# Cross-attention layer: keys and queries of a head in every fourth partition, filled by 7 transfers over 128 partitions

## The chip, the cores and the metric

The kernel runs on 1 core of one Trainium2 chip. The metric is the device time of one execution in microseconds (us), as the median of several runs. Engines: TensorE (PE, its weight loads PEld), VectorE (DVE), ScalarE (ACT), GpSimd (POOL) and SyncE (SP). SP and ScalarE each issue DMA transfers on a queue of their own; the 16 DMA engines serve both.

## The reference

One layer of cross-attention with an MLP: 8 batches of 256 queries and 1601 keys, width 256, 16 heads of width 16, all in f32.

```
x = layer_norm(hidden, ln1_w, ln1_b)
q = heads(x @ q_w + q_b); k = heads(ctx @ k_w + k_b); v = heads(ctx @ v_w + v_b)
attn = softmax(where(mask, q k^T / sqrt(16), -max))
hidden = merge(attn v) @ cproj_w + cproj_b + hidden
out = hidden + gelu(layer_norm(hidden, ln2_w, ln2_b) @ fc_w + fc_b) @ proj_w + proj_b
```

## The kernel before, in words

*Split products.* Keys and queries are held as a high part that TensorE's short format (fp32r) represents exactly and a low rest. A score is q_hi k_hi + q_hi k_lo + q_lo k_hi, which one product makes if the three terms are stacked along the contraction: 3 x 16 rows. Two rows come on top: row 48 (MASKROW) adds the mask (ones among the queries, the mask's large negative number among the keys), row 49 (MAXROW) subtracts a bound of the row's maximum (ones among the keys, minus the sampled maximum among the queries).

*Slots.* A batch has 4 slots (SLOTS) of 4 heads. `kst` [128, 4 slots, 2, 1664] and `qst` [128, 4 slots, 2, 256] hold them: heads j = 0, 1 of a slot in partitions 0 to 49, heads j + 2 in partitions 64 to 113 (HALF = 64), so that the products of two heads use the two halves of TensorE's array. Both are SBUF tensors; the other partitions are not used.

*The way of the keys.* k_unit multiplies a chunk of the context (4 chunks of 384, 384, 384 and 449 keys) by the key weights into a PSUM bank, for two groups of 8 heads (mt = 0, 1). k_evac on VectorE (lines 725 and 728) makes the high and low part in kpart. store_k on SP (line 386) writes them to k_scr in HBM: 4 stores per group of heads, 384 or 449 KB each. q_evac and store_q (line 392) do the same for the queries. `fill` then reads a slot from k_scr and q_scr into kst and qst: in each half, 32 partitions of keys (hi and lo, line 348), 16 partitions of keys (hi again, line 349), 1 partition of mask (line 351), 32 partitions of queries (hi twice, by a broadcast of 2 copies) and 16 of queries (lo, both line 355): 10 transfers in all (FILLS). The order of heads and widths in k_scr is set on the host by `by_width`, which reorders the columns of the weights.

*The maxima.* max_unit (line 1106) multiplies a sample of queries with a sample of keys of a slot, 49 rows deep; it waits for the slot's fill (slot_in). VectorE reduces it (lines 771, 774), turns it to rows (line 785), and SP sends the rows to MAXROW of qst (send_rows, line 398, 4 transfers). Only then may the scores of this slot begin.

*The stream.* For each batch 52 steps (STEPS = 4 slots x 13 tiles of 128 keys), in 26 pairs: scores (line 1119, 4 products per step, 50 rows deep, into S), ScalarE's exponential (line 583, 128 x 1024 into pr), values (line 1126). Between them, at pairs given in tables (K_AT, V_AT, MAX_AT, Q_AT and others), TensorE makes the next batch's keys, values and queries (line 1056, 1093) and the maxima. Slots 2 and 3 of batch 0 have their sampled products at pairs 3, 5, 9 and 11 of batch 0 itself; slot 0 and 1 ahead of the stream.

*Order in the head.* Each engine runs a list written by hand. SP: loads, the mask, six transfers of constant rows (constant_rows, lines 407 to 411: mask rows beyond key 1601, ones of MAXROW in kst, ones of MASKROW in qst), store_k(0, 0, 0 to 3), store_q(0), half 0 of slot 0's fill, store_k(0, 1, 0 to 3), rows of slots 0 and 1, slot 3's fill, then per batch. ScalarE: copies of the context to its high part (line 571), the loads of batch 1's context (next_ctx, line 340), half 1 of slot 0's fill, slot 1's fill, slot 2's fill, then the exponentials. A fill of batch 0 (first_fill) waits for the stored queries (q_out), for the stored keys of its group (k_landed: the 4 stores of mt = 0 for slots 0 and 1, all 8 for slots 2 and 3), for the mask and the constant rows. GpSimd: small memsets (line 494: the columns of kst beyond key 1601), c_low (line 515), c_high of later batches (line 510).

A second run of the whole computation stands under `failed(...)`, for maxima that proved too low; it isn't entered here.

Of the kernel before, what the change touches and what calls it, by code (L numbers as in the profile page):

```python
# [42 lines left out]
H, HD = 16, 16  # L43
# [17 lines left out]
CHUNK = [c for c in range(CH) for _ in range(NT[c])]  # L61
HALF = P // 2
NJ = HG // 2
MASKROW, MAXROW = 3 * HD, 3 * HD + 1
KROWS = MAXROW + 1
SCALE = 1.0 / float(np.sqrt(HD))
EPS = 1e-5
# [106 lines left out]
def build(nc, x, ctx_t, mask, w_kv, w_qc, fc, pj, cols, rows, ident, out):  # L174
    stack = ExitStack()
    with stack:
# [3 lines left out]
        def sem(name):  # L180
            return stack.enter_context(nc.semaphore(name))
# [95 lines left out]
        ln_steps, ln_root = sem("ln_steps"), sem("ln_root")  # L277
        good_steps, good_ready, flag_done = map(sem, ("good_steps", "good_ready", "flag_done"))
        xn_done, xb_done, xagain_done = map(sem, ("xn_done", "xb_done", "xagain_done"))
        o_zeroed, again_zeroed = sem("o_zeroed"), sem("again_zeroed")  # L280
        mlpw_hi, mlpw_lo = sem("mlpw_hi"), sem("mlpw_lo")

        kb_ready, kb_taken, mb_ready, mb_taken, xb_ready, xb_taken = map(
# [56 lines left out]
            eng.dma_start(cT[:, c, :, 0:NK[c]], ctx_t[b, :, :, T0[c] * P:T0[c] * P + NK[c]].rearrange("k p t -> p k t")  # L340
                          ).then_inc(ctx_in[c], 16)

        def fill(eng, s_, b, s, halves=range(2)):

            rows_of = k_scr[bass.ds(b, 1), s // 2].rearrange("o r (d h) t -> (o r d) h t", h=HM)
            for g_ in halves:
                r0, h0 = g_ * HALF, HG * (s % 2) + NJ * g_
                eng.dma_start(kst_d[r0:r0 + 2 * HD, s, :, 0:LK], rows_of[:, h0:h0 + NJ, 0:LK]).then_inc(s_.slot_in[s], 16)
                eng.dma_start(kst_d[r0 + 2 * HD:r0 + 3 * HD, s, :, 0:LK], rows_of[0:HD, h0:h0 + NJ, 0:LK]
                              ).then_inc(s_.slot_in[s], 16)  # L350
                eng.dma_start(kst_d[r0 + MASKROW:r0 + MASKROW + 1, s, :, 0:LK],
                              mask_scr[bass.ds(b, 1), :].unsqueeze(1).broadcast_to([1, NJ, LK])
                              ).then_inc(s_.slot_in[s], 16)
                for r, copies in ((0, 2), (1, 1)):
                    eng.dma_start(qst_d[r0 + 2 * HD * r:r0 + 2 * HD * r + copies * HD, s, :, :].rearrange("p j q -> p (j q)"),
                                  q_scr[bass.ds(b, 1), s // 2, r].rearrange("o (d h) q -> o d (h q)", h=HM)[
                                      :, :, h0 * LQ:(h0 + NJ) * LQ].broadcast_to([copies, HD, NJ * LQ])
                                  ).then_inc(s_.slot_in[s], 16)

        FILLS = 10  # L360
        ROWS_IN = 16 * HG

        def k_landed(eng, units):
# [3 lines left out]

        UK = 2 * CH

        def first_fill(eng, b, s, halves=range(2)):  # L370

            eng.wait_ge(q_out, 32 * (b + 1))
            k_landed(eng, UK * b + CH * (s // 2 + 1))
            if b == 0:
                eng.wait_ge(mask_out, 16)
                eng.wait_ge(ones_in, 16 * 6)
            else:
                eng.wait_ge(first.scores_done, STEPS * (b - 1) + KT * (s + 1))
            fill(eng, first, b, s, halves)

        @block.sync
        def _(sp):
            def store_k(b, mt, c):
                u, t, n = UK * b + CH * mt + c, T0[c] * P, NK[c]
                sp.wait_ge(kb_taken, k_use(b, mt, c) + 1)
                sp.dma_start(k_scr[b, mt, :, :, t:t + n].rearrange("r p t -> p r t"),
                             kpart[:, u % KBUF, :, 0:n].bitcast(F32)).then_inc(k_out[u % KBUF], 16)

            def store_q(b):
                sp.wait_ge(ql_done, b + 1)  # L390
                for mt in range(2):
                    sp.dma_start(q_scr[b, mt].rearrange("r p q -> p r q"), qpart[:, mt, :, :].bitcast(F32)
                                 ).then_inc(q_out, 16)
# [11 lines left out]
            def constant_rows():  # L405
                for r0 in (0, HALF):
                    sp.dma_start(kst_d[r0 + MASKROW:r0 + MASKROW + 1, :, :, LK:KP].rearrange("p s j t -> p (s j) t"),
                                 ones[0:1, 0:KP - LK].unsqueeze(1).broadcast_to([1, SLOTS * NJ, KP - LK])).then_inc(ones_in, 16)
                    sp.dma_start(kst_d[r0 + MAXROW:r0 + MAXROW + 1, :, :, :].rearrange("p s j (n t) -> p (s j n) t", t=P),
                                 ones[1:2, 0:P].unsqueeze(1).broadcast_to([1, SLOTS * NJ * KT, P])).then_inc(ones_in, 16)  # L410
                    sp.dma_start(qst_d[r0 + MASKROW:r0 + MASKROW + 1, :, :, :].rearrange("p s j t -> p (s j) t"),
                                 ones[1:2, 0:LQ].unsqueeze(1).broadcast_to([1, SLOTS * NJ, LQ])).then_inc(ones_in, 16)
# [13 lines left out]
            sp.wait_ge(some_out, 16)  # L426
            sp.dma_start(some[:], some_scr[0].partition_broadcast(P)).then_inc(some_in, 16)

            sp.wait_ge(pads_set, 3)
            constant_rows()  # L430

            for c in range(CH):
                store_k(0, 0, c)
            store_q(0)
            first_fill(sp, 0, 0, [0])
            for c in range(CH):
                store_k(0, 1, c)
            first_rows(0, 0)
# [31 lines left out]
            with failed(sp):  # L470
                for s in range(SLOTS):
                    sp.sem_inc(whole.mrow_in[s], ONE)
                sp.wait_ge(pads_set, 11)
                constant_rows()
                sp.wait_ge(ones_in, 16 * 12)
                sp.dma_start(hid[:], x.rearrange("n p d -> p n d")).then_inc(xagain_in, 16)
                with sp.Fori(0, B) as b:
                    sp.wait_ge(whole.h_steps, ONE + b)
                    for s in range(SLOTS):
                        fill(sp, whole, b, s)  # L480
                        sp.dma_start(vsl[:, 0, s, :, :].rearrange("p t w -> p (t w)"),
                                     v_scr[bass.ds(b, 1), :, s, :].rearrange("o p w -> (o p) w")).then_inc(whole.slot_in[s], 16)
                    for s in range(SLOTS):
                        sp.wait_ge(max_taken, ONE + USES * (SLOTS * b + s + 1))
                        send_rows(whole, b, s)
                store_out(whole)

        @block.gpsimd
        def _(pool):
# [1 line left out]
            nc.gpsimd.memset(ones[:], 1.0).then_inc(pads_set, 1)  # L491
            pool.wait_ge(pads_set, 1)
            nc.gpsimd.memset(ones[0:1, :], -MASKED).then_inc(pads_set, 1)
            nc.gpsimd.memset(kst_d[:, :, :, LK:KP], 0.0).then_inc(pads_set, 1)
            nc.gpsimd.memset(cT[:, CH - 1, :, NK[-1]:NKM], 0.0).then_inc(pads_set, 1)

            def v_pads(par, before):
# [55 lines left out]
            y_low(first)  # L553
            with failed(pool):
                pool.wait_ge(first.pj_ready, TOK)
                nc.gpsimd.memset(kst_d[:, :, :, LK:KP], 0.0).then_inc(pads_set, 1)
                pool.wait_ge(xagain_in, 16)
                nc.gpsimd.tensor_tensor(hid[:], hid[:], bc_s.unsqueeze(1).broadcast_to([P, TOK, D]), ALU.add
                                        ).then_inc(xagain_done, 1)
                y_low(whole)  # L560

        @block.scalar
        def _(act):
# [5 lines left out]
            def high(c):  # L569
                act.wait_ge(ctx_in[c], 16)  # L570
                nc.scalar.activation(c_hi[:, c, :, 0:NKE[c]], cT[:, c, :, 0:NKE[c]], ACT.Copy).then_inc(hi_done, 1)  # L571
# [59 lines left out]
            x_root(0, 2 * QT, XA_VAR)  # L631
            for c in range(2, CH):
                high(c)
            for c in range(CH):
                next_ctx(1, c)
            first_fill(act, 0, 0, [1])
            first_fill(act, 0, 1)
            first_fill(act, 0, 2)
            for b in range(B):
# [411 lines left out]
        def _(pe):  # L1051
# [45 lines left out]
            def max_unit(b, s, j, kb, mb):  # L1097

                if j == 0:
                    pe.wait_ge(first.slot_in[s], 16 * FILLS * (b + 1))  # L1100
                bank_free(mb_taken, mb)
                bank_free(kb_taken, kb)
                for q in range(QT):
                    for g_, (bank, ready) in enumerate(((MB[:, :], mb_ready), (KB, kb_ready))):
                        rows_ = slice(g_ * HALF, g_ * HALF + MASKROW + 1)
                        last = nc.tensor.matmul(bank[:, q * SAMPLE:(q + 1) * SAMPLE], query_set(rows_, s, j, q),  # L1106
                                                kst[rows_, s, j, q * SAMPLE:(q + 1) * SAMPLE], start=True, stop=True)
                        if q == QT - 1:
                            last.then_inc(ready, 1)
# [173 lines left out]
            def all_maxima(n, b, s):  # L1283
                pe.wait_ge(whole.slot_in[s], 16 * (FILLS + 1) * (b + 1))
                for h in range(HG):
                    g_, j = h // NJ, h % NJ
                    rows_ = slice(g_ * HALF, g_ * HALF + MASKROW + 1)
                    for i, (q, k, w) in enumerate(ALLKEYS):
                        pe.wait_ge(max_taken, ONE + USES * n + h * len(ALLKEYS) + i)
                        nc.tensor.matmul(MB[:, 0:w], query_set(rows_, s, j, q), kst[rows_, s, j, k:k + w],  # L1290
                                         start=True, stop=True).then_inc(max_ready, 1)
# [64 lines left out]
```

## Time and profile before

| | us |
|---|---|
| median of 3 runs | 773.13 |
| lowest and highest | 768.25, 775.28 |
| the profiled execution | 768.76 |
| its span, first to last instruction | 767.0 |
| PE busy in it | 702.5 (92%) |
| PEld busy | 478.5 (62%) |
| ACT busy | 446.1 (58%) |
| DVE busy | 371.3 (48%) |
| POOL busy | 120.9 (16%) |

Queue q1 (SP) moved 80.47 MB in 40700 packets, q10 (ScalarE) 32.17 MB in 10494. How to read it: busy time of PE is modelled, and a share over the whole span is a mean over stretches with different limits. PEclk is the clock granted to TensorE as a share of 2.4 GHz, so 0.50 is 1.2 GHz. The DMA share is the mean over 16 engines. Lines named Lnnn are those of the kernel below; "SPq" and "ACTq" are issues of DMA transfers. "idle before ... <-X" says what ended an engine's idle time.

### The profile page before, as it was taken

How to read it: one execution, taken by the hardware profiler on the slowest of the kernel's cores; microseconds unless marked ns; L12 is line 12 of the kernel's file. 1: busy time of each engine (PE TensorE's matmuls, PEld its weight loads, DVE VectorE, ACT ScalarE, POOL GpSimd, SP SyncE). 2: the span in 40 equal slices, each digit the busy share in tenths (PEclk: the TensorE clock that was granted, in tenths of full speed). 3: DMA queues.
4: the chain of work that ended last, by engine and by line, in shares of the span. 5: the costliest groups of instructions: out<-in, count | busy, mean ns of one | idle time of the engine just before them, and what ended most of it. 6: DMA issues, size and time to landing. Idle time of an engine off the chain costs nothing.

```text
span 767.0 us, 16866 instructions
## 1 busy us (share of the span) xinstructions
PE 702.5 (92%) x7026; PEld 478.5 (62%) x7026; DVE 371.3 (48%) x824; ACT 446.1 (58%) x475; POOL 120.9 (16%) x90
## 2 busy tenths in 40 slices
PE   3657699899999999999999999999998978999997
PEld 3545466566656656666566566656664544597897
DVE  6643355265436534643464446534642331467663
ACT  3004366856676677567756775676566788733321
POOL 5222002200220032003201220131000600110010
PEclk9867799999999999999999999999999989999999
DMA  9787578657874788477938694878475800000000
GB/s 312 216 186 131 186 184 188 179 138 183 189 203 128 174 188 217 143 180 158 235 123 203 148 246 123 192 153 230 132 165 126 253 6 2 1 21 8 29 28 31
DMA packets 51275, 113.78 MB, mean 148 GB/s; under 512 B 7050, under 2 KB 40178, under 8 KB 49914
## 3 DMA queue, kind: packets, MB, share of 16 engines
q1 hardware_dynamic: 40700, 80.47, 44.5%
q10 hardware_dynamic: 10494, 32.17, 13.8%
q8 instruction: 58, 0.95, 0.6%
q14 instruction: 23, 0.19, 0.1%
HBM read 65.30 MB, written 47.06 MB: 146 GB/s over the span
## 4 chain that ended last, share of the span: by engine, by line
PE 76%; ACT 13%; DMA 5%; DVE 3%; issue 2%; ACTq 1%; DVEq 0%
PE O L1126 21%; PE S L1119 16%; ACT pr L583 11%; PE O L1056 10%; PE XB L1056 10%; PE O L1213 6%; PE S L1056 6%; DMA k_scr<-kpart 2%; DMA qst<-q_scr 2%; PE XB L1093 2%; PE XB L1153 2%; PE MB L1106 2%; DVE kpart L725 1%; DVE kpart L728 1%; DMA cols_s<-in_cols 1%
## 5 line engine op out<-in xcount | busy, mean ns | idle before, releaser
L583 ACT ACTIVATE pr<-S 128x1024 f32<-128x1024 f32 x416 | 400.6, 1024 | 188.6 <-PE S L1119 184.4
L1126 PE MATMUL O<-pr,vsl 128*17 128x256 f32 x3328 | 227.4, 388 | 1.3 <-DVE ot L790 1.3
L1119 PEld LDWEIGHTS S<-qst,kst 50*128 50x128 f32 x1664 | 117.1, 188 | 120.4 <-ACT pr L583 81.4
L1119 PE MATMUL S<-qst,kst 50*128 50x256 f32 x1664 | 171.7, 315 | 18.7 <-ACT pr L583 15.0
L1126 PEld LDWEIGHTS O<-pr,vsl 128*17 128x17 f32 x3328 | 75.3, 97 | 79.2 <-issue 17.7
L725 DVE TENSOR_SCALAR kpart<-O,cols_s 128x384 fp32r<-128x384 f32 x64 | 40.6, 635 | 120.7 <-PE O L1056 120.7
L771 DVE TENSOR_REDUCE mx<-MB 128x2 fp32r<-128x512 f32 x64 | 44.1, 690 | 79.0 <-PE MB L1106 79.0
L510 POOL CAST c_hi<-cT 128x768 fp32r<-128x768 f32 (+1 forms) x28 | 23.9, 852 | 348.0 <-DMA cT<-in_ctx_t 235.8
L1056 PE MATMUL XB<-w_hi,c_hi 128*128 128x256 f32 (+1 forms) x208 | 68.3, 328 | 2.1 <-DVE vsl L739 1.3
L739 DVE TENSOR_TENSOR vsl<-XB,rows_s 128x256 f32<-128x256 f32 (+1 forms) x104 | 43.3, 417 | 55.1 <-PE XB L1056 55.1
L1056 PE MATMUL O<-c_hi,w_hi 128*128 128x384 f32 (+1 forms) x128 | 52.6, 411 | 17.7 <-POOL c_lo L515 10.3
L515 POOL TENSOR_TENSOR c_lo<-cT,c_hi 128x768 fp32r<-128x768 f32 (+1 forms) x32 | 60.9, 1904 | 8.9 <-ACT c_hi L571 6.7
L1056 PE MATMUL XB<-w_lo,c_hi 128*128 128x256 f32 (+1 forms) x208 | 60.5, 291 | 0.0
L1056 PE MATMUL XB<-w_hi,c_lo 128*128 128x256 f32 (+1 forms) x208 | 60.1, 289 | 0.0
L601 ACT ACTIVATE g<-S,cols_s 128x512 f32<-128x512 f32 x32 | 22.1, 690 | 57.1 <-PE S L1056 52.8
L790 DVE STREAM_TRANSPOSE ot<-O 128x256 f32<-128x256 f32 x32 | 14.4, 450 | 78.0 <-PE O L1126 77.2
L1056 PEld LDWEIGHTS XB<-w_hi,c_hi 128*128 128x128 f32 (+1 forms) x208 | 40.1, 193 | 17.3 <-issue 9.0
L1056 PE MATMUL O<-c_lo,w_hi 128*128 128x384 f32 (+1 forms) x128 | 45.7, 357 | 0.0
L1056 PE MATMUL O<-c_hi,w_lo 128*128 128x384 f32 (+1 forms) x128 | 45.5, 355 | 0.0
L1106 PE MATMUL MB<-kst,qst 49*128 49x256 f32 x128 | 29.8, 314 | 16.3 <-DMA qst<-q_scr 16.2
L774 DVE TENSOR_REDUCE mx<-O 128x2 fp32r<-128x512 f32 x64 | 43.6, 682 | 0.0
L728 DVE SCALAR_TENSOR_TENSOR kpart<-O,cols_s,kpart 128x384 fp32r<-128x384 f32 x64 | 40.6, 635 | 2.3
(100 smaller groups left out, 825.6 us busy)
## 6 DMA issues: line engine op xcount, KB each, us to landing
kst<-k_scr SPq DMA_DIRECT2D x59, 400.2 KB
k_scr<-kpart SPq DMA_DIRECT2D x48, 384.0 KB, 8.0
v_scr<-vsl ACTq DMA_DIRECT2D x8, 1768.0 KB, 11.9
kst<-k_scr SPq DMA_DIRECT2D x59, 200.1 KB
cT<-in_ctx_t ACTq DMA_DIRECT2D x21, 384.0 KB, 7.6
k_scr<-kpart SPq DMA_DIRECT2D x16, 449.0 KB, 7.1
q_scr<-qpart SPq DMA_DIRECT2D x16, 256.0 KB, 2.5
qst<-q_scr SPq DMA_DIRECT2D x59, 64.0 KB
```

Of the source, the lines that this page charges most:

```text
L515: nc.gpsimd.tensor_tensor(c_lo[:, c, :, 0:n], cT[:, c, :, 0:n], c_hi[:, c, :, 0:n].bitcast(F32), ALU.subtract).then_inc(lo_done, 1)
L583: nc.scalar.activation(pr[:, n % PBUF, :], S[:, 2 * (n % 2):2 * (n % 2) + 2, :] .rearrange("p a n -> p (a n)"), ACT.Exp).then_inc(s_.exp_d ...
L725: nc.vector.tensor_scalar(kpart[:, i, 0, 0:n], KB[:, 0:n], bk_s[:, mt:mt + 1], None, ALU.add).then_inc(kh_done, 1)
L728: nc.vector.scalar_tensor_tensor(out=kpart[:, i, 1, 0:n], in0=KB[:, 0:n], scalar=bk_s[:, mt:mt + 1], in1=kpart[:, i, 0, 0:n].bitcast(F32), ...
L739: nc.vector.tensor_tensor(vsl[0:m, b % 2, :, kt, :].rearrange("p s (h w) -> p s h w", w=VW)[:, :, :, 0:HD], XB[0:m, 0:D].rearrange("p (s h ...
L771: nc.vector.tensor_reduce(mx[:, s % 2, :, j], MB[:, :].rearrange("p (q k) -> p q k", q=QT), AX.X, ALU.max, negate=True).then_inc(mb_taken, 1)
L774: nc.vector.tensor_reduce(mx[:, s % 2, :, NJ + j], KB.rearrange("p (q k) -> p q k", q=QT), AX.X, ALU.max, negate=True).then_inc(kb_taken, 1)
L1056: last = nc.tensor.matmul(dst, a, c, start=i == 0, stop=i == len(terms) - 1)
L1106: last = nc.tensor.matmul(bank[:, q * SAMPLE:(q + 1) * SAMPLE], query_set(rows_, s, j, q), kst[rows_, s, j, q * SAMPLE:(q + 1) * SAMPLE], ...
L1119: last = nc.tensor.matmul(S[:, 2 * (n % 2) + g_, j * LQ:(j + 1) * LQ], kst[rows_, s, j, kt * P:(kt + 1) * P], qst[rows_, s, j, :], start=T ...
L1126: last = nc.tensor.matmul(O[32 * h:32 * h + VW, 0, 0:LQ], vsl[:, par, s, kt, h * VW:(h + 1) * VW], pr[:, n % PBUF, h * LQ:(h + 1) * LQ], s ...
L1213: last = nc.tensor.matmul(O[:, n % 2, 0:D], w[:, i, cut], v[:, i, :], start=i == 0 and m == 0, stop=i == NI - 1 and m == 2)
```

## The change

The three parts of keys and queries no longer stand one behind the other. A half array's partition 4 d + part holds dimension d of part 0, 1 or 2 (PARTS = 4), the two halves together every fourth partition of all 128. Part 3's partitions are zero but for two: partition 3 of a half is MASKROW, partition 63 MAXROW. A fill is 3 transfers of 32 partitions for the keys, 3 for the queries and 1 of two partitions for the mask. The products are 64 rows deep (sampled ones 63). For the zeros GpSimd clears all of qst (2048 columns) where it cleared the last columns of kst (504), and ScalarE writes kst by 8 copies of 1664 zeros from qst; SP's constant rows wait for them and go behind store_k(0, 0, 0 to 3). SP issues two of slot 0's transfers and ScalarE the five others, where each issued a half.

```diff
-MASKROW, MAXROW = 3 * HD, 3 * HD + 1
+PARTS = HALF // HD
+MASKROW, MAXROW = PARTS - 1, HALF - 1
 KROWS = MAXROW + 1
...
+        def fill_k(eng, s_, b, s, parts):
+            rows_ = slice(HALF * (s % 2), HALF * (s % 2 + 1))
+            for part in parts:
+                eng.dma_start(kst_d[part::PARTS, s, :, 0:LK],
+                              k_scr[bass.ds(b, 1), s // 2, part % 2, rows_, 0:LK].rearrange("o (p j) t -> (o p) j t", j=NJ)
                               ).then_inc(s_.slot_in[s], 16)
+        def fill_q(eng, s_, b, s):
+            rows_ = slice(HALF * (s % 2), HALF * (s % 2 + 1))
+            for part, r in enumerate((0, 0, 1)):
+                eng.dma_start(qst_d[part::PARTS, s, :, :].rearrange("p j q -> p (j q)"),
+                              q_scr[bass.ds(b, 1), s // 2, r, rows_, :].rearrange("o (p j) q -> (o p) (j q)", j=NJ)
                               ).then_inc(s_.slot_in[s], 16)
+        def fill_mask(eng, s_, b, s):
+            eng.dma_start(kst_d[MASKROW::HALF, s, :, 0:LK],
+                          mask_scr[bass.ds(b, 1), :].unsqueeze(1).broadcast_to([2, NJ, LK])).then_inc(s_.slot_in[s], 16)
+        def fill(eng, s_, b, s):
+            fill_k(eng, s_, b, s, range(PARTS - 1))
+            fill_q(eng, s_, b, s)
+            fill_mask(eng, s_, b, s)
-        FILLS = 10
+        FILLS = 7
...
@@ sync
-            sp.wait_ge(pads_set, 3)
-            constant_rows()
             for c in range(CH):
                 store_k(0, 0, c)
+            sp.wait_ge(pads_set, 3)
+            sp.wait_ge(kst_zeroed, SLOTS * NJ)
+            constant_rows()
             store_q(0)
-            first_fill(sp, 0, 0, [0])
+            fill_ready(sp, 0, 0)
+            fill_k(sp, first, 0, 0, [0, 1])
...
@@ gpsimd
-            nc.gpsimd.memset(kst_d[:, :, :, LK:KP], 0.0).then_inc(pads_set, 1)
+            nc.gpsimd.memset(qst_d, 0.0).then_inc(pads_set, 1)
...
@@ scalar
             for c in range(2, CH):
                 high(c)
+            zeros = qst_d.rearrange("p s j q -> p (s j q)")[:, 0:KP]
+            for s in range(SLOTS):
+                for j in range(NJ):
+                    nc.scalar.activation(kst[:, s, j, :], zeros, ACT.Copy).then_inc(kst_zeroed, 1)
             for c in range(CH):
                 next_ctx(1, c)
-            first_fill(act, 0, 0, [1])
+            fill_ready(act, 0, 0)
+            fill_k(act, first, 0, 0, [2])
+            fill_q(act, first, 0, 0)
+            fill_mask(act, first, 0, 0)
             first_fill(act, 0, 1)
             first_fill(act, 0, 2)
...
@@ tensor, sampled products
-                        rows_ = slice(g_ * HALF, g_ * HALF + MASKROW + 1)
+                        rows_ = slice(g_ * HALF, g_ * HALF + MAXROW)
...
@@ host
     def by_width(a):
-        return a.reshape(*a.shape[:-1], 2, HM, HD).swapaxes(-1, -2).reshape(a.shape)
+        return a.reshape(*a.shape[:-1], H // NJ, NJ, HD).swapaxes(-1, -2).reshape(a.shape)
```

## Rows read from the trace of the kernel before

**Rows 1.** Stretches: length, busy us (PE, PEld, DVE, ACT, POOL), PE clock, DMA share, GB/s
```profile
0.00:83.00 83.00, 43.25 (x244) 35.76 (x244) 39.14 (x78) 16.40 (x17) 24.67 (x28) 0.81 0.82 208
83.00:95.00 12.00, 12.00 (x98) 7.93 (x98) 6.33 (x12) 3.99 (x5) 0.00 (x0) 0.74 0.53 208
95.00:665.00 570.00, 551.64 (x6074) 349.46 (x6073) 262.50 (x605) 396.48 (x413) 89.03 (x59) 0.99 0.65 161
```

**Rows 2.** Sum of waits: total us, times, longest us
```profile
PE MB L1106 <- DMA qst<-q_scr: 16.2, 3, 6.7
```

**Rows 3.** TensorE in order of time, 44 to 84 us: start, us
```profile
49.61 0.58 PE L1106 MATMUL MB<-kst,qst 49*128 49x256 f32 x1 [5.38 <-DMA qst<-q_scr]
...
60.70 0.58 PE L1106 MATMUL MB<-kst,qst 49*128 49x256 f32 x1 [4.16 <-DMA qst<-q_scr]
...
65.24 0.81 PE L1119 MATMUL S<-qst,kst 50*128 50x256 f32 x8
...
75.46 0.74 PE L1119 MATMUL S<-qst,kst 50*128 50x256 f32 x8
82.88 0.58 PE L1106 MATMUL MB<-kst,qst 49*128 49x256 f32 x1 [6.68 <-DMA qst<-q_scr]
```

**Rows 4.** Chain that ended last, 40 to 84 us: start, us, what
```profile
42.84 18.23 DMA k_scr<-kpart
...
61.31 0.32 ACTq L348
...
66.17 16.66 DMA qst<-q_scr
```

**Rows 5.** ScalarE in order of time: start, us
```profile
5.98 1.54 ACT L628 ACTIVATE pr<-pr 8x1601 f32<-8x1601 uint8 x1 [1.34 <-DMA cols_s<-in_cols]
...
14.66 0.94 ACT L571 ACTIVATE c_hi<-cT 128x900 fp32r<-128x900 f32 x1
...
66.93 1.28 ACT L583 ACT_TABLE_LOAD   x1 [51.33 <-issue]
68.22 1.94 ACT L583 ACTIVATE pr<-S 128x1024 f32<-128x1024 f32 x2
```

**Rows 6.** Busy time by stretch, columns as in rows 1
```profile
4.00:20.00 16.00, 7.51 (x36) 6.90 (x36) 12.81 (x30) 6.83 (x8) 8.02 (x6) 1.00 1.06 358
36.00:52.00 16.00, 8.46 (x42) 7.34 (x42) 5.42 (x11) 0.00 (x0) 2.67 (x2) 0.71 1.03 228
56.00:60.00 4.00, 0.55 (x3) 0.25 (x2) 0.42 (x1) 0.00 (x0) 0.00 (x0) 0.50 0.13 44
64.00:80.00 16.00, 10.48 (x94) 7.51 (x93) 5.62 (x12) 8.94 (x9) 4.34 (x3) 0.93 1.02 153
```

**Rows 7.** Groups of instructions by form: busy us, mean ns, idle before
```profile
L571 ACT ACTIVATE c_hi<-cT 128x768 fp32r<-128x768 f32 x3 | 2.5, 834 | 2.2 <-DMA cT<-in_ctx_t 2.2
...
L494 POOL MEMSET kst<- 128x504 f32 x1 | 0.5, 512 | 0.0
```

**Rows 8.** SP's issues in order of time, 18 to 36 us: start, us
```profile
18.95 0.80 SPq L407 DMA_DIRECT2D kst<-ones  x1
...
23.62 3.61 SPq L386 DMA_DIRECT2D k_scr<-kpart  x4
31.19 0.89 SPq L392 DMA_DIRECT2D q_scr<-qpart  x2
34.11 0.35 SPq L348 DMA_DIRECT2D kst<-k_scr  x1
```

**Rows 9.** GpSimd in order of time, 8 to 12 us: start, us
```profile
8.40 1.80 POOL L515 TENSOR_TENSOR c_lo<-cT,c_hi 128x768 fp32r<-128x768 f32 x1 [3.86 <-ACT c_hi L571]
```

**Rows 10.** Weight loads by form: busy us, mean ns
```profile
L1119 PEld LDWEIGHTS S<-qst,kst 50*128 50x128 f32 x1664 | 117.1, 188 | 120.4 <-ACT pr L583 81.4 <-issue 38.7
...
L1056 PEld LDWEIGHTS XB<-w_lo,c_hi 128*128 128x128 f32 x192 | 37.9, 198 | 0.2
```

**Rows 11.** Chain that ended last, at 96 us: start, us, what
```profile
96.50 0.70 PE XB L1056 x6
```

More of the change, by code:

```diff
@@ L279, in build @@
         xn_done, xb_done, xagain_done = map(sem, ("xn_done", "xb_done", "xagain_done"))
-        o_zeroed, again_zeroed = sem("o_zeroed"), sem("again_zeroed")
+        o_zeroed, again_zeroed, kst_zeroed = sem("o_zeroed"), sem("again_zeroed"), sem("kst_zeroed")
         mlpw_hi, mlpw_lo = sem("mlpw_hi"), sem("mlpw_lo")
@@ L341, in load_ctx @@
                           ).then_inc(ctx_in[c], 16)
[L343 to L349, printed above, removed]
-                              ).then_inc(s_.slot_in[s], 16)
-                eng.dma_start(kst_d[r0 + MASKROW:r0 + MASKROW + 1, s, :, 0:LK],
-                              mask_scr[bass.ds(b, 1), :].unsqueeze(1).broadcast_to([1, NJ, LK])
-                              ).then_inc(s_.slot_in[s], 16)
[L354 to L358, printed above, removed]
@@ L368, in build, with fill_ready @@
         UK = 2 * CH
-        def first_fill(eng, b, s, halves=range(2)):
+        def fill_ready(eng, b, s):
             eng.wait_ge(q_out, 32 * (b + 1))
@@ L378, in first_fill @@
                 eng.wait_ge(first.scores_done, STEPS * (b - 1) + KT * (s + 1))
-            fill(eng, first, b, s, halves)
+        def first_fill(eng, b, s):
+            fill_ready(eng, b, s)
+            fill(eng, first, b, s)
         @block.sync
@@ L472, in _ @@
                     sp.sem_inc(whole.mrow_in[s], ONE)
-                sp.wait_ge(pads_set, 11)
+                sp.wait_ge(pads_set, 12)
                 constant_rows()
@@ L555, in _ @@
                 pool.wait_ge(first.pj_ready, TOK)
-                nc.gpsimd.memset(kst_d[:, :, :, LK:KP], 0.0).then_inc(pads_set, 1)
+                for i in range(2):
+                    pool.wait_ge(first.out_done[i], 16 * TOK // 2)
+                nc.gpsimd.memset(kst_d, 0.0).then_inc(pads_set, 1)
+                nc.gpsimd.memset(qst_d, 0.0).then_inc(pads_set, 1)
                 pool.wait_ge(xagain_in, 16)
@@ L1286, in all_maxima @@
                     g_, j = h // NJ, h % NJ
-                    rows_ = slice(g_ * HALF, g_ * HALF + MASKROW + 1)
+                    rows_ = slice(g_ * HALF, g_ * HALF + MAXROW)
                     for i, (q, k, w) in enumerate(ALLKEYS):
```

## The prediction, made blind

> **What bounds the kernel now.** I read the stretches first [rows 1]. From 95 us to 665 us TensorE has work in 551.6 of 570 us at a granted clock of 0.99, while the DMA engines are busy 0.65 of it: a faster transfer buys nothing there by itself. Before 83 us TensorE works 43 of 83 us and the DMA share is 0.82. The sum of waits names what TensorE lacks in that head [rows 2]: the first sampled products (max_unit, L1106) wait three times for a fill, 16.2 us together. The order of TensorE shows the three waits [rows 3]: it arrives at 44.2 (49.61 less 5.38), 56.5 and 76.2 us, and goes on at 49.61, 60.70 and 82.88, for slots 0, 1 and 2 of batch 0. The chain that ended last shows that the second and third are one story [rows 4]: the last store of the head, k_scr<-kpart issued at 42.84, takes 18.2 us; only then may ScalarE issue slot 2's fill (its ten transfers run from 61.31 to 66.9), and that fill lands 16.7 us after its last issue. ScalarE's first exponential waits behind these issues, at 68.22 with its table load of 1.28 us ahead of it and 51.3 us of idle time ahead of that [rows 5].
>
> **Why those fills are slow.** By shape a fill is 1.23 MB of keys, 0.20 MB of queries and 0.03 MB of mask, 1.45 MB. Three stretches and a fourth to compare them with tell it [rows 6]. From 64 to 80 us nearly only fills run: share 1.02, yet 153 GB/s. Stores and fills together make 228 GB/s (36 to 52 us). Loads over all 128 partitions at the same share make 358 GB/s (4 to 20). So the fills keep the engines busy at under half of a load's rate. And from 56 to 60 us, with slot 1 and the last store still unlanded, the share is 0.13: 0.13 x 16 = 2 engines, at 44 GB/s. Fourteen engines had nothing left, while TensorE and ScalarE waited for two.
>
> The Trainium skill names both causes. "SBUF — State Buffer", section on the DMA port swizzle, gives 27.2 GB/s for each of 16 ports, 8 ports to 32 partitions in one half and 4 to 16; two thirds of the keys at 218 and one third at 109 GB/s would be 163, and the 153 measured agrees. "DMA: Bandwidth & Descriptors", on why a DMA increments its semaphore by 16, says the slowest dimension of both patterns sets the number of engines, so the old queries' leading broadcast of 2 copies would use two; the share of 0.13 agrees. By the first, the new fill could run at up to 435 GB/s; by the second its mask still goes on two engines, its queries on sixteen.
>
> **The change, part by part.**
> 1. *Zeroing and start of the fills.* ScalarE now clears kst by 8 copies of 1664 columns. A copy of 768 columns takes 0.834 us [rows 7] and one of 900 takes 0.94 [rows 5], 0.8 ns a column, so one takes 0.834 + 896 x 0.0008 = 1.55 us and eight 12.4. They start behind the last c_hi, which ends at 15.6 [rows 5], and end at 28.0. SP waits for them before its six constant rows (issued from 18.95 to 23.6 now, 4.6 us [rows 8]), so these end at 32.6. Behind them in SP's queue stands store_q: its wait for the queries (31.19 now) is over, it goes out at 32.6, and by its present 2.9 us to the first fill (31.19 to 34.11) the fills start at 35.5 instead of 34.1: 1.4 us lost. The four store_k that now stand ahead of the constant rows leave 4 us or so sooner. Also behind the copies on ScalarE: batch 1's context (1.64 MB by shape), issued right behind the last c_hi now, by 28 then. TensorE needs it only behind the first scores (65.24 [rows 3]), so only its traffic counts: at 358 GB/s 4.6 us, largely in the gap that the earlier stores leave. I take nothing for it and keep 0 to 5 us.
> 2. *GpSimd's larger fill.* The memset goes from 504 to 2048 columns: from 0.51 us [rows 7], in proportion, 2.1, so 1.6 us more. It ends at 3.5 then, and the six small fills of vsl behind it stay as they are. ScalarE, which waits for it too, starts its first copy at 5.98 [rows 5], and GpSimd's next product waits for ScalarE until 8.40 [rows 9]. Free; without that cover 1.6 us.
> 3. *Bytes in the head.* From 35.5 us on, slots 0 and 1 (2.9 MB) and the four stores of the second half of the keys (1.64 MB) go out: 4.55 MB. Bounds for the rate: 228 GB/s, what this mixture makes now, and 358. It is nearest to the lower, since the stores and the length of a key row (6.4 KB) don't change; I take 270. Then the last lands at 35.5 + 16.9 + 1 = 53.4 us (with 228: 56.5; with 358: 49.2), where it is 61.1 now. No tail on two engines is left but 0.03 MB of mask.
> 4. *ScalarE's issues.* Ten transfers took 5.6 us, seven take 3.9: 57.3. With the table load the first exponential is at 58.7 instead of 68.22. TensorE's side is not later: slot 0 is in at 43, before its 44.2; slot 1 at about 51.7, against an arrival at 44.2 + 6.9 = 51.1 (it went from 49.61 to 56.5 for the same work); the first scores 4.5 us after that (60.70 to 65.24 [rows 3]), at 56.2.
> 5. *The third wait.* From the first exponential to the arrival at slot 2 it is 76.2 - 68.2 = 8.0 us, so TensorE arrives at 66.7. Slot 2's fill, issued from 53.4 to 57.3 with slot 3's behind it at 59, is 1.45 MB at 270: 5.4 us, in by 61. The wait of 6.7 us is gone, and what is late next is TensorE itself. Gain here: 82.88 - 66.7 = 16.2 us.
> 6. *The clock.* After the third wait the granted clock is 0.50, and over 83 to 95 us 0.74 [rows 1], 3 us lost in TensorE-bound work. Without the wait I take 2 of these back (bounds 0 and 3).
> 7. *Score products over 64 rows instead of 50, sampled ones over 63 instead of 49.* Weight loads of 50 rows take 188 ns in the mean, of 128 rows 198 [rows 10]. The rows hardly show, and most loads lie beside a product; I take 0. Upper bound, half of 1664 loads (two halves side by side) x 10 ns = 8 us; below zero there is nothing, as no row is saved.
> 8. *After 95 us.* SP issues 7 transfers instead of 10, some 1.7 us less per fill, and nothing of TensorE waits for them. 0, between 0 and 2 us gained.
>
> Sum: 16.2 + 2 = 18 us. The profiled execution took 768.76 us (span 767.0), so 750.6; it lay 4.4 below the median of 773.13, so on the median 755.
>
> **Rivals.**
> A. *The context in the way.* If batch 1's context still fills ScalarE's queue when the fills start, everything shifts by up to 4.6 us, and the gain is 13: 760. For: slot 0's ScalarE part stands behind it in one queue. Against: 7 us lie between its last issue and the first fill.
> B. *Only the tail goes.* The new partitions may get in each other's way as the old ones do: if fills stay at 228 mixed and 153 alone, the last landing is 56.5, ScalarE's issues end at 60.4, slot 2 has 1.45 MB, some 0.7 of it sharing with slot 3, so it lands near 71 instead of 61 (slot 3's is issued from 61.5 on), and TensorE waits for it at 69.7. Gain 82.9 - 71 = 12: 761. For: the rate of a fill was measured only in its old form. Against: 358 GB/s into 128 partitions.
> C. *A and B together, no change to be measured.* 12 - 5 = 7: 766.
> D. *Slower.* The two halves' products run side by side now: both L1106 products of a pair start at the same hundredth. If 64 + 63 or 64 + 64 rows filled the array so that they no longer could, a group of eight score products would take eight times the step of a whole-array product, 0.70 / 6 = 0.117 us [rows 11], 0.93 instead of 0.74 us [rows 3]: 0.2 x 208 groups = 40 us, less the 18, 795. It decides from 18 / 208 = 0.09 us per group. Against it: each half already owns 64 rows of which 50 are filled, and the second starts at row 64.
>
> **How the numbers follow.** The forecast has 0.66; A 0.13, B 0.10, C 0.06, D 0.05. A measurement of this kernel tells about 1% (7.7 us) from no change. Faster by over 1%: 0.66 + 0.13 + 0.10 = 0.89; within 1%: 0.06; slower: 0.05. The forecast's own range is from a rate of 358 with all 3 us of clock back (the first exponential then waits for the scores, at about 56.3: gain 22) to one of 228 with no clock back (gain 13): 751 to 760. The range given takes in A and B and the spread of the runs before (768.25 to 775.28): 747 to 764.
>
> **What would show it.** In the new profile: eight copies of about 1.55 us on ScalarE between 15.6 and 28; the first fill at 35.5; no stretch with share 0.13; over 250 GB/s where two fills run; the first exponential near 58.7 and the sampled products of slot 2 near 67 with no wait before them; the stretch behind that, up to the end, as long as now. It is wrong if one of the L1106 waits stays at several us, if score groups of eight take over 0.8 us, or if the first fill starts after 40 us.

## The result, and the profile after

The changed kernel took 747.62 us (median of 4 runs, 746.23 to 751.03) beside 770.69 for the kernel before, a ratio of 0.970 with a 95% interval of 0.964 to 0.977, which is a gain of 23 us, between 17.5 and 28. Run again, five times beside the kernel before on one chip, it took 748.82 beside 767.23: 0.975, 0.973 to 0.978, a gain of 18.4 us. The forecast was a gain of 18 us and 755 us, in a range of 747 to 764. The absolute number is 6 to 7 us lower than forecast mostly because the kernel before measured 767 to 771 here, not 773. The second measurement has more runs and the narrower interval (16.6 to 21.0 us), and the first includes 18 us too, so the text goes by 18.4.

The profiled execution of the changed kernel has a span of 745.4 us, 21.6 less than before. By stretch (columns as in rows 1):

```profile
0.00:83.00 83.00, 60.23 (x405) 47.75 (x406) 49.03 (x98) 36.13 (x33) 26.48 (x28) 0.88 0.74 250
83.00:95.00 12.00, 12.00 (x135) 8.00 (x132) 7.63 (x18) 8.00 (x9) 0.00 (x0) 1.00 0.65 214
95.00:665.00 570.00, 551.70 (x6010) 353.91 (x6011) 267.45 (x614) 394.64 (x414) 91.58 (x60) 0.99 0.45 155
```

Against [rows 1], TensorE works 60 us of the first 83 instead of 43, and after 95 us nothing has changed but the DMA share, 0.45 instead of 0.65: the fills got faster where nobody waits for them too. SP's issues, which answer to [rows 8]:

```profile
18.86 5.91 SPq L401 DMA_DIRECT2D k_scr<-kpart  x4
27.31 0.80 SPq L422 DMA_DIRECT2D kst<-ones  x1
...
31.31 0.65 SPq L426 DMA_DIRECT2D qst<-ones  x1
32.01 0.95 SPq L407 DMA_DIRECT2D q_scr<-qpart  x2
36.38 1.57 SPq L348 DMA_DIRECT2D kst<-k_scr  x2
```

ScalarE in order of time, from its copies of zeros to the first exponential, beside [rows 5]:

```profile
13.81 0.91 ACTq L341 DMA_DIRECT2D cT<-in_ctx_t  x2
...
15.29 1.57 ACT L656 ACTIVATE kst<-qst 128x1664 fp32r<-128x1664 f32 x1
...
19.73 7.50 ACT L656 ACTIVATE kst<-qst 128x1664 fp32r<-128x1664 f32 x5
...
53.02 1.87 ACTq L348 DMA_DIRECT2D kst<-k_scr  x3
...
57.46 1.28 ACT L602 ACT_TABLE_LOAD   x1 [30.23 <-issue]
58.76 1.94 ACT L602 ACTIVATE pr<-S 128x1024 f32<-128x1024 f32 x2
```

TensorE at the places of [rows 3]: a wait of 1.14 us for slot 0, none for slot 1 at 52.68, the first scores at 57.22, and slot 2's sampled products right behind a group of scores, with no wait:

```profile
45.82 0.58 PE L1132 MATMUL MB<-kst,qst 63*128 63x256 f32 x1 [1.14 <-DMA kst<-mask_scr]
...
52.68 0.58 PE L1132 MATMUL MB<-kst,qst 63*128 63x256 f32 x1
...
57.22 1.22 PE L1145 MATMUL S<-qst,kst 64*128 64x256 f32 x8
...
66.51 0.74 PE L1145 MATMUL S<-qst,kst 64*128 64x256 f32 x8
67.12 0.36 PE L1132 MATMUL MB<-kst,qst 63*128 63x256 f32 x1
```

And the DMA engines in four stretches, beside [rows 6]. With fills and stores in flight they make up to 420 GB/s over 4 us, where the kernel before made 202 to 235 in the like stretches (228 on the mean of [rows 6]), and no stretch of two engines at 0.13 is left:

```profile
40.00:44.00 4.00, 2.47 (x14) 2.20 (x15) 2.22 (x5) 0.00 (x0) 2.29 (x2) 1.00 0.94 280
44.00:48.00 4.00, 2.86 (x16) 2.33 (x14) 1.71 (x3) 0.00 (x0) 0.00 (x0) 0.64 1.05 420
48.00:52.00 4.00, 3.39 (x15) 2.78 (x15) 2.29 (x6) 0.00 (x0) 2.64 (x2) 0.50 0.68 254
52.00:56.00 4.00, 4.00 (x19) 3.10 (x19) 2.25 (x5) 0.00 (x0) 0.00 (x0) 0.50 0.41 118
```

### The profile page after: what moved, and what is told of

Read it like the earlier page. It is cut to its first block, busy times and chain, and to the rows that moved or that the text cites. A ratio compares the mean times of both kernels' runs of the same rounds, so it can differ in the third digit from the quotient of the medians.

```text
span 745.4 us, 16779 instructions
## 1 busy us (share of the span) xinstructions
PE 698.3 (94%) x7026; PEld 476.8 (64%) x7026; DVE 370.6 (50%) x824; ACT 457.9 (61%) x483; POOL 122.8 (16%) x90
## 4 chain that ended last, share of the span: by engine, by line
PE 77%; ACT 13%; issue 1%; DVE 1%; ACTq 0%; DVEq 0%
PE O L1152 22%; PE S L1145 16%; ACT pr L602 12%; PE XB L1082 11%; PE O L1082 10%; PE O L1239 6%; PE S L1082 6%; PE XB L1179 2%; PE MB L1132 2%; PE XB L1119 2%; PE XB L1111 0%; ACT pj_raw L610 0%; ACT L602 0%; PE O L1132 0%; DVE g_lo L921 0%
## 5 line engine op out<-in xcount | busy, mean ns | idle before, releaser
L1152 PE MATMUL O<-pr,vsl 128*17 128x256 f32 x3328 | 224.8, 384 | 1.3 <-DVE ot L816 1.3
L1145 PEld LDWEIGHTS S<-qst,kst 64*128 64x128 f32 x1664 | 116.0, 186 | 117.4 <-ACT pr L602 79.1
L1145 PE MATMUL S<-qst,kst 64*128 64x256 f32 x1664 | 170.5, 313 | 16.9 <-ACT pr L602 13.5
L620 ACT ACTIVATE g<-S,cols_s 128x512 f32<-128x512 f32 x32 | 22.1, 690 | 57.2 <-PE S L1082 52.9
L800 DVE TENSOR_REDUCE mx<-O 128x2 fp32r<-128x512 f32 x64 | 43.6, 681 | 0.0
L1082 PEld LDWEIGHTS O<-c_hi,w_hi 128*128 128x128 f32 x128 | 25.0, 195 | 26.2 <-issue 12.8
```

The lines of the kernel that those rows point to most:

```text
L800: nc.vector.tensor_reduce(mx[:, s % 2, :, NJ + j], KB.rearrange("p (q k) -> p q k", q=QT), AX.X, ALU.max, negate=True).then_inc(kb_taken, 1)
L1082: last = nc.tensor.matmul(dst, a, c, start=i == 0, stop=i == len(terms) - 1)
L1145: last = nc.tensor.matmul(S[:, 2 * (n % 2) + g_, j * LQ:(j + 1) * LQ], kst[rows_, s, j, kt * P:(kt + 1) * P], qst[rows_, s, j, :], start=T ...
L1152: last = nc.tensor.matmul(O[32 * h:32 * h + VW, 0, 0:LQ], vsl[:, par, s, kt, h * VW:(h + 1) * VW], pr[:, n % PBUF, h * LQ:(h + 1) * LQ], s ...
```

## The experiments

Two reasons had been given for the slow fills: the tail on two engines, and the rate of the old shape of transfer. The first four runs share a chip on which the kernel before took 767.40 us; the last three share one with 767.23. Where a run is set against the changed kernel in the first four, its ratio of 0.975 from the second set stands for it: 748.5 us.

**1. The tail alone removed.**

```diff
-                for r, copies in ((0, 2), (1, 1)):
-                    eng.dma_start(qst_d[r0 + 2 * HD * r:r0 + 2 * HD * r + copies * HD, s, :, :].rearrange("p j q -> p (j q)"),
-                                  q_scr[bass.ds(b, 1), s // 2, r].rearrange("o (d h) q -> o d (h q)", h=HM)[
-                                      :, :, h0 * LQ:(h0 + NJ) * LQ].broadcast_to([copies, HD, NJ * LQ])
-                                  ).then_inc(s_.slot_in[s], 16)
+                for part, r in enumerate((0, 0, 1)):
+                    eng.dma_start(qst_d[r0 + HD * part:r0 + HD * part + HD, s, :, :].rearrange("p j q -> p (j q)"),
+                                  q_scr[bass.ds(b, 1), s // 2, r].rearrange("o (d h) q -> (o d) (h q)", h=HM)[
+                                      :, h0 * LQ:(h0 + NJ) * LQ]
+                                  ).then_inc(s_.slot_in[s], 16)
-        FILLS = 10
+        FILLS = 12
```

> The kernel before with one edit: a half's queries come by three transfers of 16 partitions instead of one of 32 (with a leading broadcast of 2 copies) and one of 16; 12 transfers a fill. Everything else, the places of the rows too, as before. Theory (most of the head's loss was the tail on two engines that this broadcast makes): the stretch with a DMA share of 0.13 goes, the last store of the head lands near 54 us instead of 61.1, the first exponential is near 62 (two issues more per fill), the wait for slot 2 is gone or under 2 us, and the run gains 10 to 14 us. Rival (the rate of the old fills, 153 GB/s alone, is the loss): the last store lands at 58 or later, the wait for slot 2 stays at 4 us or more, and the gain is 4 us or less.

Measured: 757.76 us, ratio 0.986 (0.984 to 0.988), 9.6 us gained. The stretches behind the first fill, which starts at 36.9 here:

```profile
52.00:56.00 4.00, 1.62 (x6) 1.35 (x6) 0.78 (x3) 0.00 (x0) 0.41 (x1) 0.50 0.97 189
56.00:60.00 4.00, 2.27 (x10) 1.85 (x10) 1.29 (x2) 0.00 (x0) 0.00 (x0) 0.50 0.32 98
60.00:64.00 4.00, 4.00 (x21) 3.19 (x21) 2.26 (x5) 0.00 (x0) 1.46 (x2) 0.50 1.00 174
64.00:68.00 4.00, 3.36 (x16) 2.98 (x14) 1.66 (x3) 2.74 (x3) 1.59 (x1) 0.64 1.04 164
```

The share stays at 0.97 until nearly the end, no 0.13; but the rate is the old one, 164 to 189 GB/s. (One stretch, 44 to 48 us, made 312, so a stretch of mixed stores and fills says little by itself; the mean from 95 us on is the better sign, below in run 3.) The last store lands at 58.9, 22.1 us behind the first fill, where it was 27.0 before (34.1 to 61.1). The third wait is gone, slot 1's is still 3.6 us. The gain lies just below what the theory of the tail gave, and well above its rival's 4; but the store landed where the rival had it (58 or later), and the first exponential came at 66.55, not 62. Part of that is this profile: its first fill starts 2.8 us later than before, and it took 759.29 us, 1.5 over the median. By the medians the tail was about half of the loss, not most.

**2. The tail put back into the changed kernel.**

```diff
+                src = q_scr[bass.ds(b, 1), s // 2, r, rows_, :]
+                src = (src.rearrange("o (a p j) q -> (o a) p (j q)", a=2, j=NJ) if part < 2 else
+                       src.rearrange("o (p j) q -> (o p) (j q)", j=NJ))
```

> The changed kernel with one edit: two of the three query transfers of a fill get their source as a leading dimension of 2, as the broadcast of the kernel before had; same bytes, same partitions. Theory of the tail: a stretch of share near 0.13 comes back ahead of the last store's landing, the store lands 4 to 7 us later than in the changed kernel (52.9), and the run is 5 to 12 us slower than the changed kernel. Rival (rate): the tail is back in the share, but the time is within 3 us of the changed kernel.

Measured: 748.86 us, ratio 0.975 (0.973 to 0.977): the time of the changed kernel. The tail is back, but short:

```profile
44.00:48.00 4.00, 2.66 (x20) 2.19 (x20) 2.63 (x6) 0.00 (x0) 0.65 (x1) 1.00 1.05 420
48.00:52.00 4.00, 2.04 (x16) 1.55 (x12) 2.27 (x5) 0.00 (x0) 2.00 (x2) 1.00 0.79 295
52.00:56.00 4.00, 3.51 (x18) 2.92 (x19) 2.29 (x4) 0.00 (x0) 0.00 (x0) 0.61 0.20 50
```

The last store lands 17.5 us behind the first fill, 0.9 later than in the changed kernel (16.6; 16.0 in its second profile), not the 4 to 7 that the theory of the tail gave. The rival holds here. Together with run 1: taking away the tail alone is worth 9.6 us, taking away the slow rate alone 18.5, both together 18.4. They are not two terms of a sum. A reading that fits, but was not measured engine by engine: at the old rate the two overloaded engines were far behind when the others had finished, at the new one they have nearly caught up. The change also sends the stores of the first half of the keys 4.8 us sooner (18.86 instead of 23.62); that is no third cause of weight, since before too they had landed when the first fill began (a DMA share of 0.06 from 30 to 32 us).

**3. Key transfers by half array, still every fourth partition.**

```diff
+                for g_ in range(2):
+                    half_rows = slice(HALF * (s % 2) + 2 * HD * g_, HALF * (s % 2) + 2 * HD * (g_ + 1))
+                    eng.dma_start(kst_d[HALF * g_ + part:HALF * (g_ + 1):PARTS, s, :, 0:LK],
+                                  k_scr[bass.ds(b, 1), s // 2, part % 2, half_rows, 0:LK].rearrange("o (p j) t -> (o p) j t", j=NJ)
+                                  ).then_inc(s_.slot_in[s], 16)
-        FILLS = 7
+        FILLS = 10
```

> The changed kernel with each of the three key transfers cut in two of 16 partitions, one per half array (10 transfers a fill, every fourth partition of one half). Theory A (a transfer must span both halves to be fast): two running fills fall back towards 153 to 230 GB/s, the DMA share from 95 us on rises from 0.45 to 0.6 or more, and the run is 3 to 8 us slower than the changed kernel. Theory B (what counts is how far apart the partitions of one transfer stand, not whether it spans both halves): the share from 95 us on stays under 0.5 and the run is within 3 us of the changed kernel, 1 to 2 us of it for ScalarE's further issues.

Measured: 755.30 us, ratio 0.983 (0.981 to 0.986), 6.8 us slower than the changed kernel. The time is what theory A gave, and the rates lie nearer to theory B's: a share of 0.50, at the edge of its "under 0.5", and no fall to 230 GB/s.

```profile
95.00:665.00 570.00, 548.80 (x5989) 350.00 (x5987) 269.40 (x612) 393.15 (x413) 89.15 (x59) 0.99 0.50 156
44.00:48.00 4.00, 1.92 (x11) 1.41 (x11) 1.86 (x4) 0.00 (x0) 0.12 (x1) 0.85 1.09 379
48.00:52.00 4.00, 3.39 (x15) 2.90 (x16) 2.07 (x5) 0.00 (x0) 2.52 (x2) 0.50 1.00 330
56.00:60.00 4.00, 4.00 (x20) 3.22 (x21) 2.25 (x5) 0.00 (x0) 1.62 (x2) 0.50 0.92 264
```

The first two of the short stretches have stores from 128 partitions in flight. In the last slot 2's fill is all but alone, and it makes 264 GB/s. In the changed kernel the same fill, alone too, makes 327:

```profile
56.00:58.00 2.00, 2.00 (x12) 1.67 (x13) 1.73 (x4) 0.54 (x1) 0.59 (x1) 0.50 0.91 327
```

Rate over share from 95 us on is 156 / 0.50 = 312 GB/s, against 155 / 0.45 = 344 in the changed kernel, 161 / 0.65 = 248 before and 158 / 0.68 = 232 in run 1. So spanning both halves is worth a part of the faster rate. The larger part came with something else that run 3 keeps, and there are two candidates: the partitions in SBUF stand four apart, and the rows that one transfer reads in HBM now stand one behind the other, where before a transfer took two rows of every eight (`by_width` changed with the fills). No run has the one without the other, so which of them it is stays open. The last store lands 17.9 us behind the first fill, 1.3 later. The rest of the 6.8 us is something else: three further issues before ScalarE's first exponential (62.01, 3.3 later than 58.76 in all), and three batches of 75.2 to 75.4 us between their value stores where the others take 74.3, 3 us more. In each of these TensorE waits once, 0.9 to 1.1 us, for a value tile, and shortly before a small operation of VectorE with two inputs lasts until a subtraction of GpSimd, begun just ahead of it, ends: 1.71 us for one of 128 x 8 at 184.24, 1.85 and 1.96 for one of 128 x 128 at 259.59 and 409.14, which take 0.12 and 0.28 otherwise. VectorE and then GpSimd in the first case:

```profile
184.24 1.71 DVE L836 SCALAR_TENSOR_TENSOR good<-ot,good 128x8 f32<-128x8 f32 x1
```

```profile
184.09 1.83 POOL L533 TENSOR_TENSOR c_lo<-cT,c_hi 128x768 fp32r<-128x768 f32 x1
```

In the changed kernel the same operation at 180.10 takes 0.50 us, until GpSimd's cast of 179.75 to 180.58 ends, and is over before GpSimd's subtraction at 180.66. GpSimd starts when the context lands, so such slips move about: one is found in the second profile of the changed kernel (75.2 us) and one each in runs 4 and 6, none in the first profile. They are no sure part of what run 3 changes.

**4. The zeros written twice.** ScalarE's eight copies are made a second time behind the first, and SP waits for sixteen.

> The changed kernel with ScalarE's 8 copies of zeros made twice, one set behind the other. Theory (copies, constant rows, stored queries and first fill are one chain): the copies end near 39.4 us instead of 27.2, the first fill starts near 48.5 instead of 36.4, and the run is 10 to 13 us slower than the changed kernel. Rival (the head is set by the bytes moved, and by then they are already waiting elsewhere): the first fill is late, but the fills then run alone and faster, and the run is 3 to 7 us slower.

Measured: 760.63 us, ratio 0.990 (0.987 to 0.993), 12.1 us slower than the changed kernel. SP's issues and TensorE's wait for slot 0:

```profile
39.37 0.80 SPq L422 DMA_DIRECT2D kst<-ones  x1
...
48.45 1.57 SPq L348 DMA_DIRECT2D kst<-k_scr  x2
```

```profile
58.46 0.58 PE L1134 MATMUL MB<-kst,qst 63*128 63x256 f32 x1 [17.54 <-DMA kst<-mask_scr]
```

The first fill starts 12.1 us later, the first exponential 12.7 (71.48), the run ends 12.1 later: from the copies to the first fill the chain holds one for one. (The edit also waits for the first eight copies before it hands over the rest, and batch 1's context leaves at 27.36 to 29.3 instead of 13.8 to 19.0; its traffic is over by about 35, long before the fills.)

**5. The changed kernel again.**

> The changed kernel itself, beside the kernel before and the next two on one chip. If the 3.3 us that came on top of the forecast are stretches of lower granted clock behind the head, and not the new fills, they differ from run to run: this profile has the first exponential within 0.5 us of 58.8 again, but the time from batch 0's value store to the end may lie anywhere from 675.8 to 680. If they are the fills' doing, that time is again 676.

Measured: 748.82 us, ratio 0.975 (0.973 to 0.978). First exponential at 58.43; from batch 0's value store to the end 676.8 us (676 in the first profile, 680.3 before). Over all profiles this stretch lies between 675.8 and 680.5 us; the two kernels with the old fills have the longest (680.3, and 680.5 in run 1), those with new fills 675.8 to 679.9. A part that differs is the 4 us behind ScalarE's table loads for the square root. Before, and after 18.3 us less:

```profile
136.00:140.00 4.00, 2.24 (x24) 1.41 (x25) 0.88 (x2) 3.96 (x6) 1.35 (x1) 1.00 0.47 116
140.00:144.00 4.00, 4.00 (x35) 2.48 (x34) 1.73 (x5) 2.61 (x4) 0.00 (x0) 0.57 0.99 161
```

```profile
117.70:121.70 4.00, 2.24 (x24) 1.41 (x25) 0.87 (x2) 3.96 (x6) 0.00 (x0) 1.00 0.65 238
121.70:125.70 4.00, 4.00 (x56) 2.31 (x56) 2.15 (x6) 3.31 (x4) 0.94 (x2) 1.00 0.02 4
```

TensorE idles the same 1.76 of 4 us in both, and behind it the granted clock falls to 1.2 GHz in the one (0.57 over the stretch) and stays at 2.4 in the other; 35 products start instead of 56. The fall is there in the kernel before and in runs 1, 2, 3 and 6, not in either profile of the changed kernel nor in runs 4 and 7. From the first table load to the next value store it takes 9.8 us without the fall, 11.2 to 11.3 with it, and 12.7 in run 1: a cost of 1.5 us, once of 2.9. Runs with and without it have the same fills, so the new fills don't prevent it; what decides it, and whether the old ones favour it (both kernels that have them show it), stays open.

**6. Slot 2's first fill by SP.** `first_fill(act, 0, 2)` goes, and SP has `first_fill(sp, 0, 2)` between the rows of slots 0 and 1.

> The changed kernel with slot 2's first fill issued by SP, between the rows of slots 0 and 1, instead of ScalarE. Theory (ScalarE's first exponential waits for its own issues, which end at 57.46, with the scores just ready at 57.8): the table is loaded long before, the first exponential is at about 57.9 instead of 58.8, and the run gains about 1 us, under what can be told. Rival (SP's seven issues of 4.3 us push slot 1's rows, which are due at 57): the rows of slot 1 leave late but are needed only at step 13, so nothing is lost; if they were, TensorE would stop before the scores of slot 1.

Measured: 748.20 us, ratio 0.974 (0.971 to 0.977), 0.6 below the changed kernel, which can't be told from nothing. The table is loaded at 45.70, the first exponential starts at 56.77 (57.9 expected), 1.7 to 2.0 us earlier than in the two profiles of the changed kernel, and slot 1's rows leave from 57.9 on without anyone waiting. This profile has the fall of the clock described above.

**7. A short start.** To run 6 it adds:

```diff
-            sp.wait_ge(pads_set, 3)
-            sp.wait_ge(kst_zeroed, SLOTS * NJ)
-            constant_rows()
             store_q(0)
+            sp.wait_ge(pads_set, 3)
+            sp.wait_ge(kst_zeroed, SLOTS * NJ)
+            query_ones()
...
-                    nc.scalar.activation(kst[:, s, j, :], zeros, ACT.Copy).then_inc(kst_zeroed, 1)
+                    nc.scalar.activation(kst[:, s, j, :], zeros, ACT.Identity, bias=one_row[:]).then_inc(kst_zeroed, 1)
...
+            pool.wait_ge(ql_done, 1)
             for b in range(1, B):
```

one_row is 1 in partitions 63 and 127 (two columns of the identity added by GpSimd), and mask_scr has 1664 columns, the last ones filled by VectorE, so that the mask's transfer covers them.

> The changed kernel, slot 2's fill by SP, and a shorter start: ScalarE's copies add a column that is 1 in MAXROW, so no constant rows are sent to kst; the mask in HBM has its columns beyond key 1601; the two rows of ones for qst go behind store_q, which waits for its queries alone; and GpSimd takes up batch 1's context only when the first queries are split (beside it VectorE's cast and subtraction took 1.08 and 2.17 us, alone 0.43 and 0.69). Theory: store_q leaves at about 29.5 instead of 32.0, the first fill at 32.5 instead of 36.4, the first exponential at about 56 and the run gains 2 to 3.5 us on the changed kernel. Rival (TensorE's own work in the head already ends it): the fill starts early, the waits before the sampled products go, and the first exponential stays at 57.5 or later.

Measured: 744.88 us (744.01 to 747.49), ratio 0.971 (0.969 to 0.974), 3.9 us below the changed kernel and 22.4 below the kernel before: the lowest median here. SP's issues and ScalarE's first exponential:

```profile
30.06 0.88 SPq L410 DMA_DIRECT2D q_scr<-qpart  x2
31.05 1.50 SPq L425 DMA_DIRECT2D qst<-ones  x2
33.97 1.31 SPq L350 DMA_DIRECT2D kst<-k_scr  x2
```

```profile
54.43 1.94 ACT L616 ACTIVATE pr<-S 128x1024 f32<-128x1024 f32 x2 [10.38 <-PE S L1160]
```

The first fill starts 2.4 us earlier and the first exponential 4.3, of which run 6 gave 2.0; as in run 6 it waits for scores, not for issues, and the rival (57.5 or later) is out. Store_q leaves at 30.06 (29.5 expected) and the first fill at 33.97 (32.5): SP waits 1.1 us of it for the two rows of ones. The run bundles four edits, and only their sum was measured. VectorE's split of the queries in the changed kernel and in this one, where GpSimd stays out of its way:

```profile
28.52 1.08 DVE L787 CAST qpart<-xn 128x512 fp32r<-128x512 f32 x1
29.64 2.17 DVE L789 TENSOR_TENSOR qpart<-xn,qpart 128x512 fp32r<-128x512 f32 x1
```

```profile
28.88 0.43 DVE L802 CAST qpart<-xn 128x512 fp32r<-128x512 f32 x1
29.34 0.69 DVE L804 TENSOR_TENSOR qpart<-xn,qpart 128x512 fp32r<-128x512 f32 x1
```

## Why the prediction was right, point by point

*The bound.* Right. The waits before 83 us were all that faster fills could win: the batches in between are 74.3 us apart before and after. (Run 7 shows that more was left in the start itself.)

*Step 1, start of the fills.* The copies cost 1.49 to 1.57 us each (1.55 forecast) and end at 27.23 (28.0); the constant rows end at 31.96 (32.6); store_q leaves at 32.01 (32.6). The first fill starts at 36.38 (35.5), because 4.4 us pass from store_q to it instead of the 2.9 of [rows 8]. That step had carried over a duration from a place where no constant rows stood right ahead of it; run 1, built as before, again has 2.9 (33.96 to 36.88), and run 4, built as after, 4.4. The term left out is the landing of the constant rows. In the changed kernel SP waits 1.9 us for them (`L387 <- DMA qst<-ones`), until 35.1, and 1.3 more for the stored queries behind them; from 30 to 32 us the DMA share is 0.45 at only 26 GB/s. In the second profile of the changed kernel (run 5) VectorE is late and store_q leaves at 33.72, yet the first fill starts at 36.66, 4.5 us behind the last constant row's issue where it was 4.4 in the first. So it is in all six profiles with the six constant rows right ahead of store_q: 4.4 to 4.5 us behind that issue, whether store_q follows at once or 1.6 us later. That they hold the first fill up is read from these rows; no run moved them alone. One statement was wrong without a price: batch 1's context is issued at 13.8 to 18.9 as before. ScalarE's queue issues transfers ahead of copies that are already handed over, so rival A had nothing to stand on.

*Step 2.* The memset took 1.80 us (2.1) and GpSimd's first subtraction started at 8.19, as before. Free.

*Step 3, the bytes.* The last store landed at 53.0 us (53.4): it started 0.9 late and took 16.6 us instead of 17.9, so two misses offset each other, and that is luck. The rate of 270 GB/s, a choice between two bounds, came out for the whole stretch (4.55 MB in 16.6 us is 274), but as a mean of something faster: 420 GB/s while all is in flight, above the 358 taken as the upper bound, and little while the stores wait for VectorE (the last is issued at about 43.6). The upper bound had been read from loads, and these transfers proved no slower; the reason given for a rate near the lower bound, that stores and row length stay, did not hold.

*Step 4.* Seven issues took 4.4 us (3.9), 0.63 each instead of 0.56; the first exponential started at 58.76 (58.7). TensorE's side was nearer than said: slot 0 was in at 45.8, not 43, and cost a wait of 1.14 us, and the first scores came at 57.22 (56.2).

*Step 5.* TensorE came to slot 2's sampled products at 67.12 (66.7) and did not wait. Against 82.88 this is 15.8 us (16.2).

*Step 6, the clock.* By batch 0's value store the lead is 17.1 us (86.71 to 69.60), by the table loads behind it 18.3 (134.78 to 116.49): 2.5 on top of the 15.8, where 2 was taken. The clock is what differs there: 0.67 from 86.7 to 90.7 before, 1.00 from 69.6 to 73.6 after. The sum of 18 is there, and the second measurement gives just that. The further 3.3 us of the two profiles' difference are counted as no term of the change, though that is argued from the spread of run 5 and not shown: 1.5 came between the table loads and the next value store, with the fall of the clock shown in run 5, and 1.5 after the last value store (172.6 to 171.1), where the clock over the first 70 us is 0.93 before and 0.95 after.

*Step 7 and rival D.* Weight loads of 64 rows take what those of 50 took [rows 10], and groups of eight score products 0.74 us as before [rows 3]:

```profile
L1145 PEld LDWEIGHTS S<-qst,kst 64*128 64x128 f32 x1664 | 116.0, 186 | 117.4 <-ACT pr L602 79.1 <-issue 37.4
```

*Rivals B and C.* B said that the rate of the fills stays. Run 1 is B made real, with the tail gone and the rate kept: forecast 12 us, measured 9.6. What spoke for B was that the old form alone had been measured; what spoke against it, the 358 GB/s of whole loads, decided.

The two rules of the Trainium skill named ahead fit the runs, with a limit each. "SBUF — State Buffer", section on the port swizzle: every fourth partition of a half reaches all eight of its ports, as 32 in a row do, and 16 in a row only four. By this, as an estimate from the page's figures, 16 partitions at a step of four in one half would go at 218 GB/s like the old 32. Run 3's fill, alone in flight and its keys' transfers alternating between the halves, made 264. So two transfers on different halves add up to some degree here, where the page's section on two DMAs gives only 6% for it; the 330 to 379 of run 3 are with stores over all 128 partitions beside them. "DMA: Bandwidth & Descriptors", on the number of engines: the two-engine share of 0.13 went with the leading dimension of 2 (run 1), and with it a share of 0.20 at 50 GB/s came back (run 2), as stated; but what it cost was 0.4 us or 9.6, by the rate of what stands beside it.

## What to carry to other kernels

Before a slow transfer is blamed for its bytes, multiply the DMA share by 16: a share of 0.13 at the end of a phase is two engines at work, and here a source whose slowest dimension was 2 did that. Try transfers whose partitions are spread over the whole array and whose rows in HBM stand together (the two came together here), and look for stretches where TensorE waits: the same fills at 1.4 times the rate (344 against 248 GB/s over the share) bought nothing in 570 us and 18 us in the head. Two causes found in one wait need not add up: try each alone and put each back alone. A small transfer is not free either: by the reading of step 1, rows of ones to single partitions held up the store behind them by 1.5 us.

## What was not expected of the hardware

- A cast and a subtraction on VectorE took 1.08 and 2.17 us beside GpSimd's cast and subtraction on tiles of 128 x 768, and 0.43 and 0.69 alone; a VectorE operation on 8 columns took 1.71 us beside GpSimd's subtraction and 0.50 beside its cast, and 0.12 in the median of its 32 instances. "SBUF — State Buffer" of the Trainium skill has it under who interferes with whom: a VectorE instruction with two inputs in SBUF contends with a GpSimd one that reads SBUF. The rows agree: the small operation lasts until GpSimd's is over, the subtraction 0.5 us beyond it. The slow cast has one input, of which that sentence does not speak. Here it stood on the way to the first fill.
- Stores and fills together reached 420 GB/s (44 to 48 us) with 6.4 KB rows of keys to 32 partitions at a time.
- Transfers issued from ScalarE leave while its own copies, older in program order, are still to come: the context's second pair left at 16.48 and 18.57, with five or more of the eight copies not yet started. A wait between the copies holds them: in run 4, which has one, the four left from 27.36 on.
